# A two-convolution kernel: nine slots for x, shifted loads and stores, and one channel's crossed half evicted by DVE

## The reference

```python
x = x + _L0_conv_ref(_gn(x), w1, w3, w5, alpha)   # alpha0*v + alpha1*dw1x1(v) + alpha2*dw3x3(v) + alpha3*dw5x5(v)
x = x + _L1_conv_ref(_gn(x), w, b)                # one 3x3 kernel for all channels, plus a bias
def _gn(v, G=32, eps=1e-05):
    g = v.reshape(B_, G, C_ // G, H_, W_)
    m = jnp.mean(g, axis=(2, 3, 4), keepdims=True)
    s = jnp.var(g, axis=(2, 3, 4), keepdims=True)
    return ((g - m) / jnp.sqrt(s + eps)).reshape(v.shape)
```

## Time and profile before

| | |
|---|---|
| median of 3 runs | 430.67 us (428.61 to 430.91) |
| profiled execution, its own time | 432.64 us |
| span of the profiled execution | 430.8 us |
| busy share of the span: PE, DVE, ACT, POOL | 74%, 74%, 71%, 61% |
| mean granted clock of PE | 0.903 of full speed |
| DMA | 69.40 MB, mean 161 GB/s |
| the chain that ended last | DVE 33%, DMA 21%, SP's queue 13%, ACT 13%, PE 9% |

### The profile page before, as it was taken

The page is one execution under the profiler, slowest core; times in us unless marked ns, Lnnn a source line. Parts: engine busy times, 40 slices in busy tenths (PEclk is TensorE's granted clock), DMA queues, the critical chain, the costliest instruction groups (busy, mean ns, idle before and its releaser), DMA issues.

```text
span 430.8 us, 12547 instructions
## 1 busy us (share of the span) xinstructions
PE 318.5 (74%) x5206; PEld 276.8 (64%) x5206; DVE 318.1 (74%) x688; ACT 304.1 (71%) x372; POOL 262.3 (61%) x206
## 2 busy tenths in 40 slices
PE   2491586754986998679894998499848989898440
PEld 2361273643986798459883897389836989897220
DVE  7861899971886998399929994889649996779620
ACT  1407257089999699939995899759993999977320
POOL 6405055058788578827885588738882788865601
PEclk9997596995999899969996999889998999999685
DMA  6689488201687769676986788676868514731965
GB/s 151 169 174 204 129 188 169 73 3 41 159 200 164 199 177 210 158 189 202 199 194 171 198 184 202 161 214 173 189 163 223 145 41 118 201 97 28 264 173 146
DMA packets 112829, 69.40 MB, mean 161 GB/s; under 512 B 4540, under 2 KB 109892, under 8 KB 112772
## 3 DMA queue, kind: packets, MB, share of 16 engines
q1 hardware_dynamic: 106088, 65.31, 60.5%
q10 hardware_dynamic: 6684, 3.29, 3.3%
HBM read 41.10 MB, written 27.48 MB: 159 GB/s over the span
## 4 chain that ended last, share of the span: by engine, by line
DVE 33%; DMA 21%; SPq 13%; ACT 13%; PE 9%; issue 4%; ACTq 2%; POOL 2%; POOLq 0%; DVEq 0%
DVE xt L697 15%; DVE stats L641 13%; DMA xt<-in_x_dram 10%; PE ps L377 8%; DMA edge_scratch<-gnX 6%; ACT gn_f L551 5%; SPq L236 5%; ACT gnX L552 4%; ACT cross L561 3%; SPq L216 3%; DMA edge_scratch<-gnY 2%; SPq L250 2%; POOL gnX L864 1%; SPq L263 1%; ACTq L244 1%
## 5 line engine op out<-in xcount | busy, mean ns | idle before, releaser
L377 PE MATMUL ps<-gnX,band 64*64 64x512 f16 x2880 | 181.6, 397 | 29.9 <-DVE xt L697 18.1
L377 PEld LDWEIGHTS ps<-gnX,band 64*64 64x64 f16 x2880 | 161.1, 188 | 46.6 <-issue 40.2
L697 DVE SCALAR_TENSOR_TENSOR xt<-ps,unscale,xt 128x512 f32<-128x512 f32 (+1 forms) x194 | 143.8, 747 | 22.9 <-PE ps L377 20.1
L641 DVE BATCH_NORM_STATS2 stats<-xt 128x6 f32<-128x384 f32 x256 | 120.9, 546 | 45.6 <-DMA xt<-in_x_dram 44.9
L377 PE MATMUL ps<-gnY,band 64*64 64x512 f16 x1728 | 116.8, 414 | 33.7 <-DVE xt L697 33.7
L864 POOL TENSOR_TENSOR gnX<-gn_f,gnX 128x768 f16<-128x768 f32 x60 | 92.7, 1545 | 60.7 <-ACT gnX L552 60.7
L377 PEld LDWEIGHTS ps<-gnY,band 64*64 64x64 f16 x1728 | 97.9, 190 | 49.1 <-ACT gnY L552 23.0
L551 ACT ACTIVATE gn_f<-xt,g_add,g_mul 128x768 f32<-128x768 f32 x120 | 122.1, 1017 | 4.9 <-DVE g_add L681 4.3
L864 POOL TENSOR_TENSOR gnY<-gn_f,gnY 128x768 f16<-128x768 f32 x60 | 92.7, 1545 | 31.0 <-ACT gnY L552 31.0
L561 ACT ACTIVATE cross<-ps,unscale 64x512 f32<-64x512 f32 x94 | 64.2, 683 | 51.0 <-PE ps L377 49.4
L873 POOL TENSOR_TENSOR xt<-xt,cross 128x512 f32<-128x512 f32 x47 | 61.7, 1315 | 57.3 <-ACT cross L561 57.2
(11 more groups left out here) (78 smaller groups left out, 97.9 us busy)
## 6 DMA issues: line engine op xcount, KB each, us to landing
out_dram<-xt SPq DMA_DIRECT2D x56, 384.0 KB, 4.8
xt<-in_x_dram SPq DMA_DIRECT2D x48, 384.0 KB, 6.4
band<-diag_scratch SPq DMA_DIRECT2D x48, 160.0 KB, 3.0
haloX<-edge_scratch SPq DMA_DIRECT2D x32, 123.4 KB
xt<-in_x_dram SPq DMA_DIRECT2D x20, 192.0 KB, 4.3
xt<-in_x_dram ACTq DMA_DIRECT2D x12, 192.0 KB, 6.0
out_dram<-xt SPq DMA_DIRECT2D x12, 192.0 KB, 4.0
haloX<-edge_scratch SPq DMA_DIRECT2D x32, 61.7 KB
```

Of the source, the lines that this page charges most:

```text
L377: mm = nc.tensor.matmul(ps[to, c, half, :], weights(rows, half), moving(rows, half), start=first, stop=last)
L641: st = nc.vector.bn_stats(stats[:, q_of(at, i) % 2, at, b, e, :], flat[:, SUB * e:SUB * (e + 1)])
L697: ev = nc.vector.scalar_tensor_tensor(out=here, in0=ps[frm, c, half, :].rearrange("h (b w) -> h b w", b=NB), scalar=unscale[rows, at:at + ...
```

## The change

- xt becomes a ring of NX = 9 slots of one unit (before: eight units in four pairs), laid out by batch. Two neighbouring units can be loaded or stored by one DMA ("joint") unless they lie at slots 8 and 0.
- Period 1 loads units 4 and 5; even period j from 2 to 10 loads units j+4 and j+5. Period 3 stores unit 0; odd period j from 5 to 15 stores units j-4 and j-3; the last units go one by one. Each batch has its own `stored` semaphore, and there are two for the loads.
- In a period SP issues x of batch 0 before the edges of gnX go out, of batch 1 between these and haloX, of batches 2 and 3 after haloX.
- NCROSS is 2: the crossed half of channel 2 of Y is evicted by DVE in two pieces of 64 partitions (units 0 to 14), between `affine` and the statistics of x, and PE's wait for `evac_done` of that channel now holds for them too. In period 16 these two pieces come after `whole_part` and `low_split`. cross has two slots, used in turn.
- halo_wX is packed: a unit and channel takes 66 columns instead of 128, since the zeros between neighbours are shared. Its clearing has 3230 fp16 elements a partition instead of 6144.
- A unit's two groups are channels 3i and 48 + 3i.

```diff
-    NX = 4
+    NX = 9
+    PRE = 4
-    NCROSS = 3
+    NCROSS = 2
-        halo_w = [sb("halo_wX", [P, NU * CG, 2, R], fp16), sb("halo_wY", [P, 2, R], fp16)]
+        halo_w = [sb("halo_wX", [P, NU * CG * (R + FAR[0]) + R - FAR[0]], fp16), sb("halo_wY", [P, 2, R], fp16)]
-        xt = sb("xt", [P, NX, NB, 2, CG, 2, W])
+        xt = sb("xt", [P, NB, NX, CG, 2, W])
-        cross = sb("cross", [P, NCROSS, NB, W])
+        cross = sb("cross", [P, 2, NB, W])
-        x_in = [sem(f"x_in{r}") for r in range(NX)]
+        x_in = [sem(f"x_in{r}") for r in range(2)]
-        stored = [sem(f"stored{r}") for r in range(NX)]
+        stored = [sem(f"stored{b}") for b in range(NB)]
         def first_channel(i, g):
-            return 4 * CG * (i // 2) + 2 * CG * g + CG * (i % 2)
+            return C // 2 * g + CG * i
         def x_of(i):
-            return xt[:, (i // 2) % NX, :, i % 2, :, :, :]
+            return xt[:, :, i % NX, :, :, :]
+        def crosses_before(i, c):
+            return crossed_to(i - 1) + sum(crossed(i, k) for k in range(c))
+        def images(t, n, g, b, units):
+            c = first_channel(n, g)
+            return t[b, c:c + units * CG, :, :].rearrange("c (e p) w -> p (c e) w", e=2)
+        def rows_of(n, g, b, units):
+            at = n % NX
+            return xt[HALVES[g], b, at:at + units, :, :, :].rearrange("p u c e w -> p (u c e) w")
+        def joint(n):
+            return n % NX + 1 < NX
+        def loaded(n):
+            return sum(128 if joint(k) else 256 for k in range(PRE, n + 1, 2) if (k - n) % 4 == 0)
+        def load(eng, n, b, units, done):
             for g in range(2):
+                eng.dma_start(rows_of(n, g, b, units), images(x, n, g, b, units)).then_inc(done, 16)
+        def store(eng, n, b, units):
+            for g in range(2):
+                eng.dma_start(images(out, n, g, b, units), rows_of(n, g, b, units)).then_inc(stored[b], 16)
...
+            def stores_in(j):
+                if j < LAG + 1:
+                    return None
+                if j == LAG + 1 or j >= NU:
+                    return j - LAG - 1, 1
+                return (j - LAG - 2, 2) if j % 2 else None
+            def loads_in(j):
+                if j == 1:
+                    return PRE
+                return j + PRE if j % 2 == 0 and 2 <= j < NU - PRE else None
+            def stores_until(n):
+                return sum(stores_in(j) is not None and sum(stores_in(j)) <= n + 1 for j in range(PERIODS))
             def in_and_out(j, batches):
-                m = (j + 3) // 2 if j % 2 else j // 2 - LAG
                 for b in batches:
-                    if j % 2 and 2 <= m < NU // 2:
-                        if m >= NX:
-                            sp.wait_ge(stored[m % NX], 128 * (m // NX))
-                        load_pair(sp, m, b)
-                    elif j % 2 == 0 and m >= 0:
-                        unit_ready(2 * m + 1)
-                        store_pair(sp, m, b)
-                    elif j == PERIODS - 1:
-                        unit_ready(LAST - 1)
-                        store_unit(sp, LAST - 1, b)
+                    if stores_in(j) is not None:
+                        n, units = stores_in(j)
+                        unit_ready(n + units - 1)
+                        store(sp, n, b, units)
+                    n = loads_in(j)
+                    if n is not None:
+                        if n + 1 >= NX:
+                            sp.wait_ge(stored[b], 32 * stores_until(n + 1 - NX))
+                        if joint(n):
+                            load(sp, n, b, 2, x_in[n // 2 % 2])
+                        else:
+                            for k in range(n, n + 2):
+                                load(sp, k, b, 1, x_in[n // 2 % 2])
...
-                in_and_out(j, (0, 1))
+                in_and_out(j, (0,))
                 if j + 1 < NU:
                     edges_out(sp, X, j + 1)
-                in_and_out(j, (2,))
+                in_and_out(j, (1,))
                 if j + 1 < NU:
                     edges_in(sp, X, j + 1)
-                in_and_out(j, (3,))
+                in_and_out(j, (2, 3))
...
             def cross_over(i, c):
                 act.wait_ge(conv_done[Y], 4 * CG * i + 4 * (c + 1))
-                if i >= 1:
-                    act.wait_ge(cross_added, NCROSS * (i - 1) + min(c, NCROSS - 1) + 1)
+                k = crosses_before(i, c)
+                if k >= 2:
+                    act.wait_ge(cross_added, k - 1)
...
-            nc.vector.memset(halo_w[X][:, :, :, :], 0.0).then_inc(halo_w_zero, 1)
+            nc.vector.memset(halo_w[X][:, :], 0.0).then_inc(halo_w_zero, 1)
```

More of the change, by code:

```diff
@@ L239, in edges_in @@
                        .then_inc(halo_in[s][p], 16)
-        def load_unit(eng, n, b, done):
+        def images(t, n, g, b, units):
[9 more added lines that the diff above has]
+        def load(eng, n, b, units, done):
             for g in range(2):
[L243 to L247, removed]
+                eng.dma_start(rows_of(n, g, b, units), images(x, n, g, b, units)).then_inc(done, 16)
+        def store(eng, n, b, units):
             for g in range(2):
[L249 to L265, removed]
+                eng.dma_start(images(out, n, g, b, units), rows_of(n, g, b, units)).then_inc(stored[b], 16)
         @block.sync
@@ L276, in _ @@
             for b in range(2, NB):
-                load_unit(sp, 0, b, x_first_in[b])
+                load(sp, 0, b, 1, x_first_in[b])
             def save_runs(rows, to, done):
@@ L311, in _ @@
             for b in range(NB):
-                load_unit(sp, 1, b, x_unit_in[0])
+                load(sp, 1, b, 1, x_unit_in[0])
             edges_out(sp, X, 0)
@@ L323, in _ @@
             for b in range(NB):
-                load_unit(sp, 3, b, x_unit_in[2])
+                load(sp, 3, b, 1, x_unit_in[2])
             def unit_ready(n):
@@ L355, in _ @@
                     edges_in(sp, Y, y)
-                in_and_out(j, (0, 1))
+                in_and_out(j, (0,))
                 if j + 1 < NU:
                     edges_out(sp, X, j + 1)
-                in_and_out(j, (2,))
+                in_and_out(j, (1,))
                 if j + 1 < NU:
                     edges_in(sp, X, j + 1)
-                in_and_out(j, (3,))
+                in_and_out(j, (2, 3))
             unit_ready(LAST)
             for b in (0, 1):
-                store_unit(sp, LAST, b)
-            for r in range(NX):
-                sp.wait_ge(stored[r], 256 if r < NX - 1 else 384)
+                store(sp, LAST, b, 1)
+            for b in range(NB):
+                sp.wait_ge(stored[b], 32 * (stores_until(LAST) + 1))
         @block.tensor
@@ L425, in edge @@
                     pe.wait_ge(halo_in[s][i % 2], halo_landed(i))
+                far = R + FAR[X]
                 def used(rows):
                     return slice(rows.start, rows.start + HROWS[s])
-                tiles(s, c, lambda rows, half: halo_w[s][used(rows), CG * i + c, half, :] if s == X else halo_w[s][used(rows), half, :],
+                tiles(s, c, lambda rows, half: halo_w[s][used(rows), far * (CG * i + c) + R * half:far * (CG * i + c) + R * half + R] if s == X else halo_w[s][used(rows), half, :],
                       lambda rows, half: halo[s][used(rows), i % 2, :, c, 0:W], False, True)
@@ L455, in of_half @@
                     def of_half(t):
-                        return t[:, 0:C].rearrange("k (m g u) -> k m g u", g=2, u=2 * CG)[:, :, g, :]
+                        return t[:, C // 2 * g:C // 2 * (g + 1)]
                     for q in range(4):
@@ L523, in _ @@
             for b in range(2):
-                load_unit(act, 0, b, x_first_in[b])
+                load(act, 0, b, 1, x_first_in[b])
             act.wait_ge(const_ready, 3)
@@ L557, in cross_over @@
                 act.wait_ge(conv_done[Y], 4 * CG * i + 4 * (c + 1))
-                if i >= 1:
-                    act.wait_ge(cross_added, NCROSS * (i - 1) + min(c, NCROSS - 1) + 1)
+                k = crosses_before(i, c)
+                if k >= 2:
+                    act.wait_ge(cross_added, k - 1)
                 for to, frm in ((LO, HI), (HI, LO)):
-                    cr = nc.scalar.activation(cross[to, c, :, :].rearrange("p b w -> p (b w)"), ps[frm, c, 1, :], ACT.Identity,
+                    cr = nc.scalar.activation(cross[to, k % 2, :, :].rearrange("p b w -> p (b w)"), ps[frm, c, 1, :], ACT.Identity,
                                               scale=unscale[frm, NU * CG:NU * CG + 1])
@@ L571, in halo_weights @@
                 for q in range(4):
-                    nc.scalar.copy(halo_w[X][:, :, (1, 1, 0, 0)[q], (0, 1, R - 2, R - 1)[q]], made[:, 0:NU * CG, q])\
+                    at = (R, R + 1, R - 2, R - 1)[q]
+                    nc.scalar.copy(halo_w[X][:, at:at + (R + FAR[X]) * (NU * CG - 1) + 1:R + FAR[X]], made[:, 0:NU * CG, q])\
                       .then_inc(halo_w_ready, 1)
@@ L582, in _ @@
             for b in range(NB):
```

(12 more changed lines are left out.)

## The result

The changed kernel takes 466.41 us (median of 4 runs, 464.78 to 467.58), the kernel before in the same job 430.79 (428.61 to 431.78): a ratio of 1.083, interval 1.078 to 1.089.

The account below looks back on a forecast made before the run. The prediction took SP's round of issues and landings as the bound, DVE and ACT close behind. Middle -10.3, start -1.2 and end +1.0 sum to -10.5 us, so 430.67 becomes 420.2, range 409 to 430.

Parts of the forecast that it names:

- rival C: Change does nothing: SP's round stays 23.4 to 24 us, PE waits for halos instead; 428.5 to 433 us, chance 0.13.
- DVE's own loop, 20.7: Middle periods: two added evictions cost DVE 1.53 us, 0.35 comes back; 19.52 becomes 20.7 us a period.
- DVE's wait for x: Every second period DVE idled 7.47 us for x; loading a period further ahead was to remove that.
- SP's round, 22.9: SP's loop of issues and landings in the middle: 23.1 us storing, 22.6 loading, mean 22.9, against 22.7 before.
- The leg to haloY: First part of SP's round: two more x queue ahead, adding 1.9 us; 8.0 us in the store round.
- the saving ahead of haloX: SP's round from first x to haloX: two fewer x transfers, 3.2 us less; 7.24 in the load round.
- The slip of 3 us that PE could bear: Middle periods: SP may fall some 3 us behind compute before late halos hold PE; taken off periods 6 to 11.
- Start, -1.2: Start: halved halo_wX cuts its clearing from 2.62 to about 1.4 us, saving 1.2, at worst 0.
- The tail, +1.0: Period 16: DVE's two evictions stand behind low_split and delay PE's last channel; +1.0 us, between 0 and +3.
- A: The forecast itself: SP's round still paces the middle; 420 us, range 415 to 427, chance 0.50.
- B: DVE becomes the bound: all eleven middle periods take 20.7 us; total 410 us, chance 0.25.
- D: Slower: SP's queue fills with back-to-back x and haloX transfers, round 24.8 us; total 439 us, chance 0.12.

Follow-up runs that it names:

- the aligned one: Changed kernel plus an unused 192-byte tile per partition ahead of band5 and xt, so xt again starts on a multiple of 256 bytes: 429.13 us, ratio 0.999.
- xt 64 off: Kernel before with 64 unused bytes ahead of xt and 192 behind it, so xt alone is moved: 453.57 us, ratio 1.051.
- xt 128 off: Kernel before with 128 unused bytes ahead of band5 and xt: 439.90 us, ratio 1.024.
- gn, halo 64 off: Kernel before with 64 unused bytes behind xt, shifting gn_f, gn and halo but not band5 and xt: 430.18 us, ratio 1.002.
- best kernel: Changed kernel with the 192-byte unused tile, x at its old places in SP's order, and NCROSS 3: 419.50 us, ratio 0.975.

## Why the prediction was wrong

**The step that failed** is the sentence "Layout edits (xt by batch, packed halo weights, two cross slots, per-batch counts) keep the number, shapes and element counts of the instructions; I take nothing for them." The count and shapes were as said, and the packed halo weights still moved xt to 64 bytes past a multiple of 256. That costs 37 us in the changed kernel (466.4 against 429.1), 26 in the changed kernel with the old order (453.2 against 427.4) and 24.6 in the kernel before (453.6 against 429.0). (The pad moves band5, gn and halo with xt; in the kernel before xt alone accounts for the loss, 453.6 against 454.4 with all of them moved.) Order and placement make each other dearer. By the spans of the changed kernel and the aligned one, 10.1 us of it stand in the start (110.4 against 100.3) and 27.7 in the middle (277.1 against 249.4).

The chain, link by link: a row of x is a 512-byte packet (the traces have 98304 of that size, as many as x has rows, in and out). Worked out from the single packets of 512 bytes in the traces, in the 1.6 us ahead of each x landing, their mean time is

| ns a packet | before | xt 64 off | xt 128 off | gn, halo 64 off | after | after, aligned |
|---|---|---|---|---|---|---|
| around loads | 41.5 | 48.6 | 44.7 | 40.9 | 45.9 | 37.8 |
| around stores | 29.6 | 32.5 | 33.8 | 29.6 | 32.1 | 29.9 |

SP's round grows with them. The mean round of periods 6 to 11, taken apart by the traces of SP (26 issues in each round), is

| us a round | before | xt 64 off | after, aligned | after |
|---|---|---|---|---|
| the round | 23.15 | 25.3 | 23.7 | 26.6 |
| SP busy issuing | 18.8 | 20.2 | 19.2 | 21.3 |
| SP waiting for its own edges | 2.5 | 3.5 | 2.9 | 3.7 |

So issuing fills four fifths of SP's round, and most of what misplacement adds (1.4 of 2.1 us in the kernel before, 2.1 of 2.9 in the changed one) is issues that take longer, 724 to 777 ns and 738 to 818 ns on average. Longer waits for edges are the smaller part. That placement is the cause is shown; that it acts through the packets' time fits the tables and the landings, but no experiment changed the packet time without the place, and why slower packets should stretch SP's issues stays open. The Trainium skill ("DMA: Bandwidth & Descriptors", How a descriptor splits into AXI transactions) says that when a descriptor does not start on a multiple of 256 bytes, its first transaction begins at the boundary below, and the bytes fetched ahead of the start still cost beats of 32 bytes. The runs agree that a move of 64 bytes costs time, by 7 ns in 41 around loads. Counted that way, a start 128 bytes past a boundary is no cheaper than one 64 past it; stores agree (33.8 against 32.5 ns), loads do not (44.7 against 48.6), and the time of the kernel goes with the loads.

**Without the misplacement the forecast stood closer.** The aligned changed kernel is the fair test of the rest: 429.13, just inside the range, 8.9 above the forecast, and no faster than before: rival C. Its span of 426.5 splits like this against the forecast terms (start 107.5 - 1.2; 237.9; 37.7; 37.4 + 1.0):

| us | forecast | aligned | |
|---|---|---|---|
| to period 3 | 106.3 | 100.3 | -6.0 |
| period 3 to 14 | 237.9 | 249.4 | +11.5 |
| 14 to 16 | 37.7 | 37.9 | +0.2 |
| tail | 38.4 | 38.8 | +0.4 |

*DVE's own loop, 20.7:* right. It is seen in four periods of the aligned kernel and in four odd ones of the kernel before with two crosses. *DVE's wait for x:* gone as said, 4.5 us in the aligned kernel. *SP's round, 22.9:* mis-sized, the second step that failed. The aligned rounds of periods 6 to 11 average 23.7, and in the profile they range from 21.8 to 25.3. The leg to haloY and the saving ahead of haloX came as forecast (7.85 for 8.0, 7.45 for 7.24 even unaligned). The four stores or loads behind haloX did not: I took 3.2 us for them and 3.3 for haloX's own issue. SP's timeline of the aligned kernel has 4.42 (stores), 3.64 (loads) and 4.09 (haloX):

```profile
209.21 4.42 SPq L271 DMA_DIRECT2D out_dram<-xt  x4
...
233.24 3.64 SPq L267 DMA_DIRECT2D xt<-in_x_dram  x4
...
252.85 4.09 SPq L242 DMA_DIRECT2D haloX<-edge_scratch  x4
```

*The slip of 3 us that PE could bear:* too generous. Periods 6 to 11 took 138.9 us instead of 134.4, and period 12 26.3 instead of 20.7: SP had not caught up when x was over. Period 3 took 22.2 instead of 20.7. *Start, -1.2:* better than said once aligned (-7.2), worse when not (+2.9). Placement makes the 10.1 us between the two; which other edits give the -7.2 was not tried apart.

*The tail, +1.0:* measured +2.7, with the step incomplete. The timeline of the changed kernel's end, from its last RECIPROCAL (before: the earlier trace rows):

```profile
430.30 3.16 DVE L750 TENSOR_TENSOR gnY<-gn_f,gnY 128x768 f16<-128x768 f32 x2
...
433.50 2.29 DVE L726 SCALAR_TENSOR_TENSOR xt<-ps,unscale,xt 64x512 f32<-64x512 f32 x3
...
435.16 3.79 PE L402 MATMUL ps<-gnY,band 64*64 64x512 f16 x36 [2.38 <-DVE xt L726]
...
439.29 0.69 ACT L589 ACTIVATE cross<-ps,unscale 64x512 f32<-64x512 f32 x1 [5.00 <-PE ps L402]
...
439.37 1.34 ACTq L225 DMA_DIRECT2D edge_scratch<-gnY  x1
...
450.77 1.49 PE L402 MATMUL ps<-haloY,halo_wY 35*64 35x512 f16 x12 [5.39 <-DMA haloY<-edge_scratch]
```

The prediction followed the evictions to PE and stopped there. PE's edges come after the 36 products, ACT's copy across waits for them, and behind that copy on ACT stand the last unit's edges out. They leave 13.7 us after the RECIPROCAL; before it was 9.9:

```profile
403.33 2.01 ACTq L220 DMA_DIRECT2D edge_scratch<-gnY  x2
```

PE waits for their return at the very end. The pairs of kernels that differ in NCROSS alone put the price in the tail at 4.1 us (37.4 to 41.5) in the kernel before, and at 4.9 (33.9 to 38.8) and 3.7 (33.3 to 37.0, old order) in the aligned one. The net was smaller since the changed kernel's halo comes back in 11.4 us (439.37 to 450.77) instead of 13.1 (403.33 to 416.47). In the best kernel it takes 8.6:

```profile
396.94 1.08 ACTq L226 DMA_DIRECT2D edge_scratch<-gnY  x1
...
405.56 0.84 PE L403 MATMUL ps<-haloY,halo_wY 35*64 35x512 f16 x12 [2.47 <-DMA haloY<-edge_scratch]
```

**What each part is worth.** Placement of xt: +37 us with the new order on SP, +26 with the old. The third channel on DVE: +5.5 with the new order (423.6 to 429.1), +7.9 with the old (419.5 to 427.4) and +6.7 in the kernel before, of which the tail holds 3.7 to 4.9. The order on SP: 1.7 to 4.1 us in the aligned kernel with nine slots (427.4 to 429.1 and 419.5 to 423.6), 13 when x is not aligned, and 13 in the kernel before, where x is aligned but has only four slots of two units. Channels: 0. Nine slots with shifted joint loads and stores, and the smaller clearing, which were not taken apart: about -9 (428.6 to 419.5), by spans 5.4 of it in the start, 1.9 in the middle and 4.1 in the tail.

**The rivals.** A had the mechanism of the middle, SP's round as the pace, in the changed kernel and in the aligned one from period 7 on, and missed its size. B (DVE paces at 20.7 throughout) shows in four of the eleven periods, even aligned. C came true for the aligned kernel, in time (428.5 to 433), in kind (PE waits for haloY in place of DVE for x, lines below) and in its sum: seven rounds of 23.7 and four periods of 20.7 make 248.7, measured 249.4:

```profile
PE ps L403 <- DMA haloY<-edge_scratch: 26.2, 8, 4.9
...
DVE stats L671 <- DMA xt<-in_x_dram: 4.5, 4, 1.6
```

D named the right shape for the unaligned one, waits for halos in each period from 5 on, and a round above 23.9; it took the cause to be transfers standing back to back. With the places put right the same transfers in the same order give 23.7 a round, so that alone was not enough.

## What to carry to other kernels

When an edit changes the size of any tile, work out where every later tile starts, and keep tiles with large DMA traffic on multiples of 256 bytes (the two good places here lie a multiple of 512 apart, so no experiment separates 256 from 512; where in doubt, try the tile at a few distances of 64 bytes): one unused tile of 64 bytes cost 5.8% here, and one of 192 took 8% back. When a kernel is slower though the DMA engines are as busy and move fewer GB/s, look at the time of a packet before looking at the order. Follow a moved instruction in the tail until the last DMA that stands behind it on any queue, and test each edit of a bundle alone: here the best kernel is the change less two of its parts, plus a pad.

## What the runs showed of the hardware

- A tile's start matters for DMA with 512-byte rows: 64 bytes off the old, good place adds 17% to a packet around loads (41.5 to 48.6 ns) and 10% around stores (29.6 to 32.5). 128 bytes off adds less to loads (44.7) and more to stores (33.8).
- Off by 64 bytes, gn and halo cost nothing (ratio 1.002), although the halo is filled by DMA as well.
- DMA issues on SP are not of one price: two x take 1.36 us, but four behind haloX took 3.6 to 5.0, and haloX's four issues 2.77 in load rounds and up to 4.7 in store rounds. With xt 64 bytes off, the mean of all issues rose from 724 to 777 ns (kernel before) and from 738 to 818 ns (changed kernel).
- One engine that issues everything can be the bound by its issues: 26 of them fill 18.8 of SP's 23.15 us a round in the kernel before.
- The price of an order on a queue depends on the rest: in the kernel with nine slots the same three lines cost 13 us with slower packets and 1.7 with normal ones, but also 13 us with normal packets in the kernel before, whose x has four slots of two units.
